# Delta-rule block on one core: the second batch's tokens turned by 64 partitions, small products on eight tiles of the array

## The reference, cut to what matters

```python
xn = layernorm(x)                                    # x: [2, 4096, 512] float32
q, k, v = xn @ Wq, xn @ Wk, silu(xn @ Wv)            # 16 heads of 32
q, k = l2n(q) * 32 ** -0.5, l2n(k)
beta = sigmoid(xn @ Wb)
def step(S, t):                                      # S: [batch, head, 32, 32], 4096 steps
    delta = (v_t - k_t @ S) * beta_t
    S = S + outer(k_t, delta)
    o_t = q_t @ S
o = o * rsqrt(mean(o * o) + 1e-5) * o_norm_weight
out = x + o @ Wo + (silu(xn @ gate_w * gate_s) * (xn @ up_w * up_s)) @ down_w * down_s
```

## Time and profile before

| | |
|---|---|
| median of 3 runs | 2339.17 us (2338.87 to 2341.85) |
| the profiled execution, its own time | 2343.81 us |
| its span, first to last instruction | 2342.1 us |
| matmuls' busy time | 2235.0 us |
| VectorE's busy time | 1786.9 us |
| ScalarE's busy time | 857.9 us |
| one turn in the middle of the program (904.40 to 1045.30) | 140.90 us |

### The profile page before, as it was taken

How to read it: one execution, slowest core, us unless ns; L and a number is a source line. 1 busy time by engine, 2 the same in 40 slices (tenths; PEclk the granted TensorE clock), 3 DMA queues, 4 the chain that set the end, 5 groups by cost and what they waited for, 6 DMA issues and landing times.

```text
span 2342.1 us, 89426 instructions
## 1 busy us (share of the span) xinstructions
PE 2235.0 (95%) x40464; PEld 1228.6 (52%) x40688; DVE 1786.9 (76%) x3167; ACT 857.9 (37%) x2077; POOL 265.7 (11%) x519
## 2 busy tenths in 40 slices
PE   2899999999999999999999999999999999999996
PEld 1455555555546555455555546555455555546553
DVE  8986968778686786968768696786968768697775
ACT  4652524325242342523325242342423325242341
POOL 2101010020100101011020100101011020100100
PEclk9899999999999999999999999999999999999998
DMA  7000111101111001111001111001111001111000
GB/s 256 20 7 17 37 21 38 17 7 38 21 37 22 24 16 21 37 22 38 12 12 38 21 37 22 15 26 21 37 21 38 12 12 38 21 37 22 12 10 20
DMA packets 89978, 68.96 MB, mean 29 GB/s; under 512 B 68480, under 2 KB 68480, under 8 KB 89600
## 3 DMA queue, kind: packets, MB, share of 16 engines
q1 hardware_dynamic: 88880, 63.20, 9.6%
q10 hardware_dynamic: 720, 0.03, 0.0%
HBM read 30.72 MB, written 16.78 MB: 20 GB/s over the span
## 4 chain that ended last, share of the span: by engine, by line
PE 93%; DVE 4%; issue 2%; DMA 1%; ACT 0%; SPq 0%
PE D L440 28%; PE T L355 22%; PE D L430 22%; PE D L506 14%; PE D L371 7%; DMA qt<-in_L_attn_Wq_dram 1%; DVE outer_v L1198 1%; DVE at L1205 1%; DVE amax L935 0%; DVE kq L925 0%; DVE wd L926 0%; DVE wgu L926 0%; DVE f_hi L925 0%; DVE f_lo L925 0%; DVE qt L1383 0%
## 5 line engine op out<-in xcount | busy, mean ns | idle before, releaser
L440 PE MATMUL D<-xt,wgu 128*128 128x512 f16 x3072 | 689.6, 381 | 8.2 <-ACT sg L720 6.4
L430 PE MATMUL D<-xt,w_hi 128*128 128x512 f16 x1664 | 489.1, 380 | 24.4 <-DVE w_lo L978 24.4
L440 PEld LDWEIGHTS D<-xt,wgu 128*128 128x128 f16 x3072 | 291.9, 98 | 357.0 <-ACT sg L720 6.9
L430 PE MATMUL D<-xt,w_lo 128*128 128x512 f16 x768 | 291.9, 380 | 0.0
L1205 DVE TENSOR_TENSOR at<-at,outer_v 128x62 f32<-128x62 f32 (+15 forms) x496 | 262.2, 529 | 11.8
L1198 DVE TENSOR_TENSOR outer_v<-mt,at 128x62 f32<-128x62 f32 (+15 forms) x496 | 260.9, 526 | 13.0
L430 PEld LDWEIGHTS D<-xt,w_hi 128*128 128x128 f16 x1664 | 159.0, 98 | 212.7 <-issue 26.2
L506 PE MATMUL D<-wd,f_hi 128*128 128x512 bf16 x656 | 248.7, 379 | 17.8 <-issue 17.8
L506 PE MATMUL D<-wd,f_lo 128*128 128x512 bf16 x656 | 248.8, 379 | 16.1 <-issue 15.3
L710 ACT ACTIVATE kpv<-kpv,rk 128x32 f32<-128x32 f32 x1024 | 231.1, 307 | 1.5
L772 ACT ACTIVATE qt<-T 128x256 f32<-128x256 f32 x128 | 49.0, 383 | 465.4 <-DVE outer_p L1341 465.4
(11 more groups left out here) (173 smaller groups left out, 2597.5 us busy)
## 6 DMA issues: line engine op xcount, KB each, us to landing
xs<-_attn_hidden_states_dram SPq DMA_DIRECT2D x32, 512.0 KB, 3.5
out_dram<-xs SPq DMA_DIRECT2D x32, 512.0 KB, 3.0
fuse<-in_L_ffn_gate_w_dram SPq DMA_DIRECT2D x2, 768.0 KB, 8.3
xs<-in_L_ffn_up_w_dram SPq DMA_DIRECT2D x2, 768.0 KB, 9.1
f_hi<-in_L_ffn_down_w_dram SPq DMA_DIRECT2D x2, 768.0 KB, 10.1
f_lo<-in_L_ffn_down_w_dram SPq DMA_DIRECT2D x2, 768.0 KB, 11.7
kpv<-in_L_attn_Wk_dram SPq DMA_DIRECT2D x1, 1024.0 KB, 11.0
qt<-in_L_attn_Wq_dram SPq DMA_DIRECT2D x1, 1024.0 KB, 13.0
```

What stands on the lines that cost most here:

```text
L430: last = nc.tensor.matmul(D[bank][:, :], w[:, k, cols], xp[:, k, :], start=n == 0, stop=n == len(products) - 1)
L440: last = nc.tensor.matmul(D[bank][:, :], wgu[:, n // 2, c:c + P], (xt_hi, xt_lo)[n % 2][:, n // 2, :], start=n == 0, stop=n == 2 * KT_ - 1)
```

## The change

For batch 1 everything that is token-major (keys, values, betas, solved triangles, state) lies turned by 64 partitions: what stood in partitions 0 to 63 stands in 64 to 127 and the other way round. The feature-major data (`kq`) stay. `quads` gets a flag `turned`: for batch 1, head h's matmul goes from input partitions 32h to output partitions 32(h xor 2). So batch 0 uses the four tiles of the array on its diagonal and batch 1 four others, in the same four strips of input partitions. All small products are issued with the two batches in alternation, into two banks. The numbers of `quads`, of their hardware matmuls and of dense matmuls stay the same.

What follows from it in the code:

- `gram` becomes `grams_of(m)`, and UW runs in four sets of 16 `quads`; each set tells VectorE once, at its end (`tiled_done` by 2), where a pair told it once per half.
- Where data cross from one layout to the other, an instruction becomes one for batch 0 over 128 partitions and two of 64 partitions for batch 1 (`parts_of`): the key transposes, the sum of the betas, ScalarE's copies of odd groups in `copy_u`, the copy of the step's output.
- In the chain the query part stays in one layout and the value part in the other, so they can't add in PSUM: the product takes four blocks of 32 columns, ScalarE copies one part (three instructions), and VectorE adds the other (`add_inner`, one per step, written behind the next step's subtraction and for the last step behind `read_down`).
- Values go through silu first, on ScalarE, from PSUM to `sg` (three instructions), and are transposed by VectorE after it; `V_AT` moves three of them by one or two operations.

```diff
-            def quads(out, lhs, rhs, start=True, shared=False):
+            def quads(out, lhs, rhs, turned):
                 for h in range(QUADS):
                     s = slice(32 * h, 32 * h + 32)
-                    last = nc.tensor.matmul(out[s], lhs[s], rhs[s], start=start, stop=True, skip_group_check=shared)
+                    to = slice(32 * (h ^ 2), 32 * (h ^ 2) + 32) if turned else s
+                    last = nc.tensor.matmul(out[to], lhs[s], rhs[s], start=True, stop=True)
...
-                            last = quads(T[g % 4][:, 64 * n:64 * n + 64], both[:, 0:CHUNK], both)
-                        last.then_inc(tiled_done, 1)
+                            for b in range(BATCH):
+                                both = kq_flat.rearrange("p (n t) -> p n t", t=2 * CHUNK)[:, m * BC + b * STEPS + n, :]
+                                last = quads(T[2 * (m % 2) + b][:, 64 * n:64 * n + 64], both[:, 0:CHUNK], both, b == 1)
+                        last.then_inc(tiled_done, 2)
...
-                        for b in range(BATCH):
-                            for m in range(MS):
+                        for m in range(MS):
+                            for b in range(BATCH):
                                 pc = m * BC + b * STEPS + c
-                                last = quads(T[2 * (c % 2) + b][:, 96 * m + 32:96 * m + 96], vt[:, pc, :],
-                                             kpv[:, 0:2, pc * DH:(pc + 1) * DH], start=False, shared=True)
+                                last = quads(T[2 * (c % 2) + b][:, 128 * m + 64:128 * m + 128], vt[:, pc, :],
+                                             kpv[:, 0:2, pc * DH:(pc + 1) * DH], b == 1)
...
+        def parts_of(b):
+            return ((low_half, high_half), (high_half, low_half)) if b else ((slice(0, P), slice(0, P)),)
...
-                        nc.vector.transpose(kt[:, m * BC:(m + 1) * BC, :], kq[:, m * BC:(m + 1) * BC, 0, :]).then_inc(kt_ready, 1)
+                        for b in range(BATCH):
+                            of_b = slice(m * BC + b * STEPS, m * BC + (b + 1) * STEPS)
+                            for to, src in parts_of(b):
+                                last = nc.vector.transpose(kt[to, of_b, :], kq[src, of_b, 0, :])
+                        last.then_inc(kt_ready, 1)
...
+                        for b in range(BATCH):
+                            tokens = slice(b * SPAN_B, (b + 1) * SPAN_B)
+                            for to, src in parts_of(b):
+                                last = nc.scalar.activation(sg[to, m % 2, tokens], D[bank_of(JOB_V[m])][src, tokens], ACT.Silu, scale=w_inv[src, 2:3])
+                        last.then_inc(v_raw, 1)
...
+                    def add_inner(c):
+                        dve.wait_ge(q_out, since(STEPS, c + 1))
+                        nc.vector.tensor_tensor(ot_v[:, :, c], ot_v[:, :, c], chain_banks(c)[:, :, :, 2, :], ALU.add).then_inc(o_ready, 1)
```

More of the change, by code:

```diff
@@ L535, in all_spans @@
                         else:
[L536 removed]
+                            pe.wait_ge(u_ready, since(8, 2 * m - 2))
                         pe.nop(nofuse=True)
                         for n in range(8):
[L539 to L543, removed]
+                            for b in range(BATCH):
+                                pc = m * BC + b * STEPS + n
+                                last = quads(T[2 * (m % 2) + b][:, 64 * n:64 * n + 64], tt[:, pc // 32, :, pc % 32],
+                                             kpv[:, 1:3, pc * DH:(pc + 1) * DH], b == 1)
+                        last.then_inc(tiled_done, 2)
+                        fill(fill_uw(m), FILL_UW)
                     for c in range(STEPS):
@@ L552, in all_spans @@
                         pe.nop(nofuse=True)
-                        for b in range(BATCH):
-                            for m in range(MS):
+                        for m in range(MS):
+                            for b in range(BATCH):
                                 pc = m * BC + b * STEPS + c
-                                last = quads(T[2 * (c % 2) + b][:, 96 * m:96 * m + 64], state[:, b, m, :],
-                                             kq_flat[:, 64 * pc:64 * pc + 64], start=m == 0, shared=True)
+                                last = quads(T[2 * (c % 2) + b][:, 128 * m:128 * m + 64], state[:, b, m, :],
+                                             kq_flat[:, 64 * pc:64 * pc + 64], b == 1)
                         last.then_inc(tiled_done, 1)
@@ L771, in all_spans @@
                         act.wait_ge(ds_read, since(STEPS, c + 1))
-                        nc.scalar.activation(ot_v[:, :, c], chain_banks(c)[:, :, :, 1, :], ACT.Copy).then_inc(o_ready, 1)
+                        for b in range(BATCH):
+                            for to, src in parts_of(b):
+                                last = nc.scalar.activation(ot_v[to, b, c], chain_banks(c)[src, b, :, 1, :], ACT.Copy)
+                        last.then_inc(q_out, 1)
             all_spans()
@@ L1061, in k_to_tokens @@
                         dve.wait_ge(kwide_ready, since(MS, m + 1))
-                        nc.vector.transpose(kt[:, m * BC:(m + 1) * BC, :], kq[:, m * BC:(m + 1) * BC, 0, :]).then_inc(kt_ready, 1)
+                        for b in range(BATCH):
+                            of_b = slice(m * BC + b * STEPS, m * BC + (b + 1) * STEPS)
+                            for to, src in parts_of(b):
+                                last = nc.vector.transpose(kt[to, of_b, :], kq[src, of_b, 0, :])
+                        last.then_inc(kt_ready, 1)
                     def v_to_tokens(m):
-                        bank = full(JOB_V[m])
-                        nc.vector.transpose(group(vt, m), D[bank][:, :]).then_inc(v_raw, 1)
+                        dve.wait_ge(v_raw, since(MS, m + 1))
+                        nc.vector.transpose(group(vt, m), sg[:, m % 2, :]).then_inc(v_ready, 1)
                     def b_to_tokens():
```

62 lines of the change are left out of this document (33 added, 29 removed).

## The result

The changed kernel takes 2318.64 us (median of 4 runs, 2315.66 to 2324.54) against 2340.27 us of the kernel before, measured beside it: a ratio of 0.991, 95% interval 0.989 to 0.993. The direction was forecast; of the 179 us of the sum 22 came, and the time lies above the forecast range, which ended at 2300. The profiled execution took 2316.68 us, its span is 2315.0 us.

The account below looks back on a forecast made before the run. PE's own list was taken to set the time in all three stages. Chain 6.7, grams 3.4 and UW 1.4 us per turn over 15 turns, plus 7 for the first, gave 2160 us; range 2110 to 2300.

Parts of the forecast that it names:

- the sum: Whole kernel: 11.5 us saved per turn over 15 turns plus 7 in the first, 179 us in all.
- The double round: Small products: two old rounds fit in one of 60 ns, so 16 old rounds fall from 0.90 to 0.48 us.
- half of it: Rival, small products: two passes follow each other on the same tiles, 84 ns per `quads` for 112; 2235 us, chance 0.16.
- grams and chain: Small products outside UW: shorter by 3.4 us per turn in the grams and 6.7 in the chain.
- Stage A: Stage ahead of UW: PE 3.4 us shorter, VectorE's added work just about covered by its waits, no new wait ahead of UW.
- UW: Triangular products' stage: VectorE's list limits it, the chain can start at 14.1 us against 15.46, gain 1.4 us per turn.
- PE's new wait ahead of the chain: End of UW: PE idles for about 2 us per turn before the first chain product, released by ScalarE's `copy_u`.
- The rival without concurrency: Small products: tiles of one strip don't work together, only costs remain, +1.0 us a turn; 2355 us, chance 0.13.
- The clock: Rival, ahead of the chain: new idle time halves the clock each turn, 27 us, 2187 us; counted within the doubling's 0.62.
- The first turn: Opening turn: other waits lie ahead of UW, so it gains only the chain's part, 7 us.

Follow-up runs that it names:

- e1: Changed kernel with 14 always-met waits added per turn on TensorE, so a turn has 5120 instructions; 2275.58 us, ratio 0.972.
- e5: e1 with gram matmuls moving 32 columns instead of 64 in all turns but the first; 2262.19 us (one run).
- e2: e1 with 128 more always-met waits once, ahead of all work, shifting every turn by half a block; 2350.73 us, ratio 1.003.
- e6: e1 with VectorE's second statistics call moved behind the last read of UW instead of ahead of it; 2258.62 us, ratio 0.966.
- e8: e1 with values transposed first by VectorE out of PSUM, in three pieces, and ScalarE's silu after; 2312.45 us, ratio 0.988.
- e3: e1 with batch 1's products on the same four diagonal tiles as batch 0, all else kept, output not the reference's; 2357.23 us, ratio 1.006.

## Why the prediction was right in its sign and wrong in its size

The sum had 11.5 us per turn. e1, which differs from the changed kernel by nothing but the alignment of its list, gained 140.85 - 136.22 = 4.6. By the steps of the sum:

- **The double round, the term that was mis-sized.** I took 60 ns for eight matmuls, from the start of a product, where eight loads lie 7 ns apart. A gram set without stalls takes 1.48 us; less the fixed 0.23 that is 78 ns for eight. So 16 old rounds fell from 0.90 to 0.62 us, not to 0.48. I read the rate of issue from the first loads of a product. The first 32 matmuls do keep to it, 60 ns for eight; the other 96 take 85. Over the whole set a matmul with its load takes 9.8 ns. The rival "half of it" had 84 ns; its size was close (1.5 and 0.9 us forecast, 1.48 and 0.85 measured), its reason wasn't: that is luck. The first 32 matmuls alternate their passes in the same way at 60 ns, and half of the columns (e5) takes 13% off and not a third. In grams and chain this takes 3.4 + 6.7 down to 2.1 + 4.0 us per turn. Stage A fell by 2.1 (82.53 to 80.39), as that says.
- **What the sum did not have: the blocks of the instruction list.** Faster products use up a block sooner. Even where turns are aligned, gaps at borders rose from 10.0 to 50.2 us; in the chain's products from 8.0 to 32.9, 1.6 us per turn. That is why the chain gained 42.76 - 40.14 = 2.6 and not 4.0. No row that I had chosen shows it: in the kernel before PE's "issue" waits at L355 were 4.7 us in all. The page's row of the instruction queue and the count of a turn's list would have shown the risk.
- **The 14 instructions.** The order of both kernels shows that waits go away. I counted them as nothing. They took the turns out of step with the blocks: 2318.6 - 2275.6 = 43 us. The sign was right, but with some luck: e2 has the same products at another place and is slower than the kernel before.
- **UW.** VectorE bounds it, and PE's new wait ahead of the chain stood where I had put it, released by the `copy_u` I had named. But the start came at 15.3 us into UW (15.68 in the mean of e1), not at 14.1. The first set reports at 1.64 us, not 1.3, since it takes 1.59; VectorE's waits for the second and third set are 0.80 and 0.38 us, where I had 0.4 in all; and from the end of the last read (972.06) to the chain's first product (973.12) it is 1.06 us, where I had 0.8. The expected gain of 1.4 us became a loss of 0.1. That read and its wait could be mended by an order of two calls (e6: 1.1 us per turn).
- **Stage A.** Right: no wait ahead of UW, `o_sums` began 3.3 us into the turn (3.5 forecast), the wait ahead of the second gram's read shrank from 3.81 to 0.96 us. VectorE's list was just about covered, and e8 shows how thin that was. VectorE was idle for 19% of the span, not for 15%, since the turn was 136 to 145 us long and not 129.4.
- **The rival without concurrency** did not come, and e3 confirms its price (2357 measured, 2355 worked out). The Trainium skill says in "TensorE: Matmul & The Clock Gate", Part 3, that loads overlap with matmuls in flight only in another row group. The traces don't agree: batch 1's tiles share batch 0's row groups and the set still fell from 2.00 to 1.48 us. The Trainium skill's 4 ns of issue per tile, in the same part, was not reached in a long row either: 9.8 ns here, a load with each matmul.
- **The clock.** Before the chain, after waits of 1.2 to 1.6 us, it stayed at 1.00. It fell after some of the block stalls only: of six of 1.9 to 2.1 us in the changed kernel three were followed by 3.41 us at 0.50 (1.2 of 2.4 GHz), of 15 of 1.9 to 2.2 us in e2 eleven.

Back to the 2160 us: the slower products cost (1.3 + 2.7) x 15 = 60 us, UW's missing gain 1.5 x 15 = 23, the chain's stalls 1.6 x 15 = 24, the drift 43: 150 of the 159 us between forecast and result. The first turn, for which I had 7 us and which gained 1.4, is 6 more.

**What stays open.** What sets off a block's transfer isn't settled. In e1 a fourth gram set's block began to come 4.2 us before its border, in the slow turn of the changed kernel 2.6 us before; the number of instructions between the start of a transfer and the border differed from one case to the next, and I found no rule. So I can't say from the list alone how much a given place will cost, nor how to get rid of the last 50 us.

## What to carry to other kernels

Count the instructions of the loop on the engine that bounds the kernel, before and after: where a loop is a whole number of blocks (here 5120 = 20 x 256), an edit that adds or removes a wait can cost more than the work that it saves, and a few idle waits bring the step back. Take the rate of a long row of small products from its middle or from its whole length, never from its first, queued instructions. When an engine's bound gets faster, read the list of the next engine up to the last instruction that the first waits for: what stands ahead of it and needn't (two statistics here) turns from free to paid.

## What the runs showed of the hardware

- TensorE's instructions came in blocks of 16 KB, 256 instructions. In the changed kernel a stall inside a product ended 2.2 to 3.0 us after the start of a block's transfer, and lasted up to 2.3 us. A turn uses 20 blocks in 136 us, but a set of 128 loads and 128 matmuls a whole block in 1.3 to 1.5 us, less than these 2.2 to 3.0.
- Shifting the list by half a block cost 75 us in e1 and 36 in the kernel before, of some 2300; some 3 of each were the inserted waits themselves.
- Products of 32x32 with a load each: 13.8 ns per matmul on four tiles, 9.8 on eight, 8.5 on eight with half of the columns. On eight tiles the first 32 of a set go at 7.5, the others at 10.7.
- A stall of about 2 us, caused by instructions alone, was in 3 of 6 cases of the changed kernel and in 11 of 15 of e2 followed by 3.4 us at half the clock, which costs another 1.7 us.
